# The causal mask of an attention stage: eight identity matmuls a head on TensorE, or adds by VectorE in PSUM

## The reference, cut to what matters

```python
q = rope(x @ w_q.T);  k = rope(x @ w_k.T);  v = x @ w_v.T
att = einsum('bqhd,bkhd->bhqk', q, k) / sqrt(64)
causal = tril(ones((S, S)))          # S = 1024
att = softmax(where(causal, att, -inf))
y = einsum('bhqk,bkhd->bqhd', att, v);  t = t + y @ w_o.T
```

## Time and profile before

| what | value |
|---|---|
| median of 3 runs | 4111.8 us (4111.73 to 4115.04) |
| the profiled execution | 4112.04 us, span 4110.2 us |
| TensorE busy | 3286.9 us (80%), 21207 matmuls |
| VectorE busy | 2073.0 us (50%) |
| ScalarE busy | 1432.6 us (35%) |
| GpSimd busy | 1538.1 us (37%) |
| attention stage, first to last mask matmul | 1105.3 to 3300.4 us |

### The profile page before, as it was taken

How to read it: one execution, slowest core, us unless ns; L and a number is a source line. 1 busy time by engine, 2 the same in 40 slices (tenths; PEclk the granted TensorE clock), 3 DMA queues, 4 the chain that set the end, 5 groups by cost and what they waited for, 6 DMA issues and landing times. The chain is left out here.

```text
span 4110.2 us, 65594 instructions
## 1 busy us (share of the span) xinstructions
PE 3286.9 (80%) x21207; PEld 2369.0 (58%) x21207; DVE 2073.0 (50%) x3068; ACT 1432.6 (35%) x2244; POOL 1538.1 (37%) x1314
## 2 busy tenths in 40 slices
PE   5333333333599999999999999999999939999998
PEld 1122222222366666666666666666666629898988
DVE  2344344344555555555555555555555555565656
ACT  0000000001144444444444444444444425454545
POOL 0577777777233333333333333333333320000000
PEclk8555555555699999999999999999999969999999
DMA  3533333333455555555545455555455533343333
GB/s 85 151 94 92 91 92 92 92 91 94 120 126 121 125 122 123 124 123 124 123 122 126 122 123 124 123 124 123 122 125 122 123 95 116 108 136 109 134 108 108
DMA packets 277334, 472.28 MB, mean 115 GB/s; under 512 B 91529, under 2 KB 103833, under 8 KB 277017
## 3 DMA queue, kind: packets, MB, share of 16 engines
q1 hardware_dynamic: 249624, 395.85, 37.2%
q0 software_dynamic: 27648, 75.53, 6.2%
HBM read 243.92 MB, written 22.29 MB: 65 GB/s over the span
## 5 line engine op out<-in xcount | busy, mean ns | idle before, releaser
L1034 ACT ACTIVATE attention_probs<-attention_pss 128x896 f32<-128x896 f32 (+4 forms) x768 | 621.3, 809 | 1003.7 <-PE attention_pss L901 994.2
L412 POOL DMA_INDIRECT deform_gat<-table,deform_idx x576 | 670.5, 1164 | 208.0 <-issue 164.2
L1083 DVE TENSOR_REDUCE attention_mx<-attention_pss 128x2 f32<-128x1024 f32 (+3 forms) x520 | 520.6, 1023 | 333.0 <-PE attention_pss L923 188.0
L967 PE MATMUL attention_psY<-attention_probs,attention_xt 128*64 128x64 f32 (+7 forms) x4386 | 645.7, 408 | 0.2 <-issue 0.2
L898 PE MATMUL attention_pss<-attention_QA,attention_KA 128*128 128x512 f32 (+4 forms) x1536 | 542.0, 407 | 15.9 <-ACT attention_probs L1034 12.0
L1121 POOL TENSOR_TENSOR attention_qk<-attention_tA,attention_tB 128x512 f32<-128x512 f32 x260 | 333.8, 1284 | 543.3 <-DVE attention_tB L1098 527.7
L1541 DVE SCALAR_TENSOR_TENSOR spectral_eo<-spectral_psE,spectral_sig,spectral_eo 64x512 fp32r<-64x512 f32 x512 | 383.9, 750 | 263.8 <-ACT spectral_eo L1520 259.2
L1444 PE MATMUL spectral_psE<-spectral_tz,spectral_up 128*128 128x256 f32 (+2 forms) x3072 | 507.5, 324 | 4.6 <-DVE spectral_eo L1541 4.6
L1444 PEld LDWEIGHTS spectral_psE<-spectral_tz,spectral_up 128*128 128x128 f32 x3072 | 470.6, 188 | 45.1 <-DVE spectral_eo L1541 6.3
L480 PE MATMUL deform_psT<-kept_ident,deform_smp 128*128 128x128 f32 (+1 forms) x320 | 85.0, 431 | 479.8 <-DVE deform_smp L439 479.8
L1097 DVE TENSOR_TENSOR attention_tA<-attention_pss,attention_cosT 128x512 f32<-128x512 f32 x260 | 179.2, 689 | 552.4 <-PE attention_pss L937 463.8
(11 more groups left out here) (164 smaller groups left out, 3747.4 us busy)
## 6 DMA issues: line engine op xcount, KB each, us to landing
attention_QA<-attention_nat_h SPq DMA_DIRECT2D x520, 128.0 KB, 2.3
spectral_tz<-phis SPq DMA_DIRECT2D x128, 320.5 KB, 4.6
spectral_tz<-phis SPq DMA_DIRECT2D x128, 320.0 KB, 4.2
attention_xb<-xn SPq DMA_DIRECT2D x67, 512.0 KB, 3.5
attention_wt<-wsplit SPq DMA_DIRECT2D x67, 512.0 KB, 4.2
attention_KA<-attention_nat_h SPq DMA_DIRECT2D x260, 128.0 KB, 2.3
attention_KB<-attention_nat_h SPq DMA_DIRECT2D x260, 128.0 KB, 2.3
attention_KA<-attention_nat_l SPq DMA_DIRECT2D x260, 128.0 KB, 2.3
```

The lines of the kernel that those rows point to most:

```text
L412: pool.indirect_dma_start(gat[:, r, k, :, :].rearrange("p q c -> p (q c)"), None, d.table.rearrange("r q c -> r (q c)"), bass.IndirectOffs ...
L967: ins = pe.matmul(psY[C * half:C * half + C, c0:c1], xt[:, kt_, :], probs[:, q + c0:q + c1], start=first, stop=(j == NS - 1), skip_group_c ...
L1034: act.activation(probs[:, pstep[j]:pstep[j] + width], pss[:, slot, lead:lead + width], ACT.Exp, scale=float(E) ** -0.5).then_inc(s_act, 1)
L1083: ins = dve.tensor_reduce(mx_far[:, :, i - 4] if k0 else mx[:, :, i], scores, AX.X, ALU.max)
```

## The change

VectorE adds the mask into the diagonal block of each tile, in PSUM, after the products of the unit are complete. A new semaphore `s_masked` counts the steps, and ScalarE's exponential waits for it in place of `s_full`. The mask matmuls on TensorE go away. The mask matmuls of the "max" units (L923) stay.

```diff
+        s_masked = sem("masked")
...
                                 for p0, p1 in by_bank(c0, c1):
-                                    pe.matmul(out[:, p0:p1], kt[:, h, P * kt_:P * kt_ + P],
+                                    ins = pe.matmul(out[:, p0:p1], kt[:, h, P * kt_:P * kt_ + P],
                                               qt[:, h, q0 + p0 - c0:q0 + p1 - c0], start=(a == 0), stop=(a == 1))
-                            d0 = c0 + P * kt_ - q0
-                            ins = pe.matmul(out[:, d0:d0 + P], identb[:, :], mask_b[:, 0, :], start=False, stop=True,
-                                            skip_group_check=True)
...
                         lead, _ = columns(j)
-                        act.wait_ge(s_full, n + 1)
+                        act.wait_ge(s_masked, BODY_HEADS * NS * it + NS * h + j + 1)
...
-                    if u[0] not in BY_ACT:
+                    if u[0] not in BY_ACT or u[0] == "S":
                         dve.wait_ge(s_full, n + 1)
+                    if u[0] == "S":
+                        for kt, q0, c0, _ in columns(u[1])[1]:
+                            d0 = c0 + P * kt - q0
+                            diagonal = pss[:, slot, d0:d0 + P]
+                            ins = dve.tensor_tensor(diagonal, diagonal, mask_b[:, 0, :], ALU.add)
+                        ins.then_inc(s_masked, 1)
```

## The result

The changed kernel takes 4042.86 us (median of 4 runs, 4042.79 to 4043.32) against 4111.76 for the kernel before in the same series. The ratio is 0.9831, 95% interval 0.9814 to 0.9848: 69 us faster, where 50 were forecast; the time lies in the stated range.

What follows compares the result with a forecast made beforehand. TensorE sets the pace. Masks save 1.52 us for two heads, less 0.35 (step 3 of the even head), 0.33 (pass start) and 0.07 (end of two heads): 0.77, 64 times 49.6, so 4112.0 becomes 4062; range 4030 to 4100.

Steps and rivals of the forecast that it cites:

- The masks' worth: TensorE without 1024 mask matmuls: 0.12 us saved before a same-shape matmul, 0.07 otherwise; 1.52 for two heads, 97 in all.
- The add: VectorE's 1024 adds of 128x128 in PSUM: 0.29 us each, bounds 0.21 and 0.42.
- The delay of the exponential: ScalarE's exponential starts 0.29 us later behind a one-tile step, at most 0.58 behind a two-tile step.
- step 3 of the even head: Score buffer refill there has slack 0.29 us: mask savings of 0.31 lost, plus 0.04, so 0.35 for two heads.
- the two places that I had seen at the edge: Steps 0 and 3 of the odd head: slack 0.44 and 0.55 us, 0.08 and 0.00 left, nothing lost.
- The start of a pass: Step 0 of a pass's first head: table load leaves no slack; 0.65 us lost for four heads, 0.33 for two.
- The end of two heads: Next scores wait up to 1.09 us for the maxima row's DMA; one mask's saving lost, 0.07 us for two heads.
- the second: Rival, 16%: VectorE's add takes its upper bound, 0.42 us; 25 us saved, 4087.
- the third: Rival, 7%: the exponential becomes the pace at score buffer reuse; kernel 35 us slower, 4147.
- the fourth: Rival, 5%: masks worth little, 0.04 us each, fitting into a stall that stays; 15 us left, or 4109.
- the fifth: Rival, 2%: TensorE's clock falls as it waits more often for buffers; some 220 us added, 4280.
- the first: Rival, 6%: the delay is hidden everywhere, so all 97 us are kept; 4015.

Runs made afterwards that it cites:

- e1: Kernel before, masks still on TensorE, with ScalarE's wait for s_pv put ahead of its wait for the scores: 4105.41 us against 4113.63.
- e6: Kernel before with the 1024 score masks left out, no adds, and ScalarE's s_pv wait ahead of the scores wait (timing only): 4008.51 us, ratio 0.9742.
- e4: Changed kernel with a second VectorE add of the same shape, into a spare SBUF tile, ahead of each add: 4072.66 us, ratio 0.9901.
- e5: Changed kernel with the mask of step 3 of the even heads (64 of 1024) back on TensorE: 4029.68 us, ratio 0.9794.
- e2: Changed kernel with the table load at the start of a pass put back behind the scores and add: 4069.42 us, ratio 0.9893.
- e7: Changed kernel with TensorE's waits at the head of a pass spread over the first three units: 4019.50 us, ratio 0.9769.
- e9: Kernel before, masks on TensorE, with ScalarE's s_pv wait first and TensorE's pass-head waits spread out: 4092.48 us, ratio 0.9951.
- e3: Kernel before with the 1024 score masks left out, no adds, waits unchanged (timing only): 4025.78 us, ratio 0.9785.

## Why the prediction was right, point by point

- **The masks' worth**: 0.12 us before a matmul of the same shape, 0.07 otherwise, 97 us in all. The total is confirmed by e1 against e6 (97 us), and the prices are borne out place by place: in the traces the stretch of the two-tile step 1 with its rope unit behind it is shorter by 0.25 in e6, that of a one-tile step ahead of a max unit by 0.06 to 0.08.
- **The add**: 0.29 forecast, 0.297 measured. Of the two figures of the Trainium skill, "VectorE: DVE Perf Modes", section on the TRN2 errata, the one for an fp32 add, 0.29 us, agrees; 120 + FD cycles, 0.26 us, does not.
- **The delay of the exponential**: mis-sized. I had set the earlier end of the scores equal to the hop to ScalarE. For step 0 of the odd head the exponential came 0.82 us after the first product of KB and QB before (2428.32 to 2429.14) and comes 1.00 after it now (2386.60 to 2387.60): 0.18 later, not 0.29. In the kernel before, 0.34 passed from the start of the mask to the exponential; now the add starts about 0.20 after the last score matmul has streamed, and the hand-over to ScalarE takes 0.03 to 0.04. The scores are ready for the reader earlier by more than the hundredths that I had taken. At step 3 of the even head it is 0.25 (2421.14 to 2421.89 before, 2379.43 to 2380.43 now): there the rope product is still in the way, by 0.07, where I had added 0.04. So the two places that I had seen at the edge kept 0.10 and 0.18 us between the end of the exponential and the refill (step 3 and step 0 of the odd head, 2395.59 to 2395.69 and 2388.62 to 2388.80); the longer delay of e4 used that up.

Those rows, of before and of after (timeline):

```profile
2421.14 0.57 PE L898 MATMUL attention_pss<-attention_QB,attention_KB 128*128 128x448 f32 x2
```

```profile
2386.60 0.63 PE L899 MATMUL attention_pss<-attention_QB,attention_KB 128*128 128x512 f32 x2
...
2387.60 1.02 ACT L1032 ACTIVATE attention_probs<-attention_pss 128x1024 f32<-128x1024 f32 x1 [1.50 <-DVE attention_pss L1081]
```

- **Step 3 of the even head**: 0.35 us for two heads lost. Right: the stretch takes 2.49 us, as before the change (2.48), e5 gets 0.23 of it back.
- **The start of a pass**: wrong, and this is the step that makes the most of the difference. "There is no slack: the whole 0.29 shows" took for granted that the table load stays behind the scores. A load that the compiler places went with the waits, and the change gave it another one. Forecast: 0.65 us a pass lost. Measured, by e2 against the changed kernel: 0.83 of such a loss avoided, 27 us, where 21 had been forecast; and the kernel before had lost 8 us at this place already (e1).
- **The end of two heads**: the wait named was wrong. Rows 8 gave 1.09 us to a DMA; the matmul row beside it, which I had not read, gives 0.42 to ScalarE's exponential:

```profile
2409.61 0.73 PE L898 MATMUL attention_pss<-attention_QA,attention_KA 128*128 128x512 f32 x2 [0.42 <-ACT attention_probs L1034]
```

  At the loop head line 1004 (L1002 in the changed kernel) waits for all of ScalarE's work. That happens once a pass, and there the delay of the last add shows in full; at the other pair nothing is lost, and the mask between is saved. Forecast 0.07 for two heads, 0.14 a pass; the pass end alone now holds 0.8 (e7: 23 us for 32 passes is 0.73), part of which stood there before (e9 against e1: 12 us, 0.37 a pass). So the change added some 0.36 a pass, 11 us, against 4.5 forecast.

The sum then closes: 97 for the masks, plus 8 for the table load (e1), minus 22 for step 3 (0.35 x 64), minus 11 for the pass end, is 72 us; 69 were measured. The losses can be checked at one stroke: e6 has neither masks nor adds, and its table load stands behind the wait for `s_pv` as in the changed kernel. Stretch by stretch (medians over the passes, from the first matmul of one kind to the first of the next) the two traces agree within 0.01 us but for two places. From the first score of step 3 of an even head to the matmuls of `pv` behind max-d TensorE takes 2.68 us in e6 and 3.04 in the changed kernel; from the last `pv` group of a pass to the next scores, 1.36 and 1.70. That is 2 x 0.36 + 0.34 = 1.06 a pass, 34 us, and 34 us lie between the medians (4008.51 and 4042.86).

The size was in part luck. 48 us of loss were forecast, 21 of them at a place where nothing was lost; instead 8 us were gained there, and the pass end lost 6 more than forecast. That the time lies in the range says little about the start of a pass: e2, where the load is on the path, lies in it as well (4069).

Of the rivals, the second (an add of 0.42), the third, the fourth and the fifth (clock 1.00 in every window read) did not come; the first, delay hidden everywhere, came half true: in all places but the two named above.

## What to carry to other kernels

When a wait moves, look at what the compiler has put between the waits of that instruction: a table load of 1.28 us sat behind the wrong one here and cost 8 to 27 us by its place alone (e1 8, e3 against e6 17, e2 27). A delay is priced place by place, slack against delay, and where one buffer has no slack the old way can stay for that one. At a loop head, ask whether the wait for "everything of the pass before" is what the first unit needs.

## What the runs showed of the hardware

- VectorE adds of 128x128 in a row start 0.20 us apart, although each is recorded with 0.29 (e4, 2399.49 to 2399.69 to 2399.89); the two adds of a two-tile step in the changed kernel take 0.50 together (2380.85). The second costs a third less than the first.
- From VectorE's end to ScalarE's start passed 0.03 to 0.04 us (2380.40 to 2380.43, 2370.14 to 2370.18). From the start of the matmul behind the last score matmul to the add it was 0.20 (2369.64 to 2369.84).
- A table load starts 0.01 to 0.02 us behind the exponential before it and the exponential behind it can start 0.02 after its end: 1.28 us in all (e7, 2354.72 to 2354.73 and 2356.01 to 2356.03).
- A wait named on the weight-load row can be a wait that costs nothing: e7 shows 0.60 us on it beside a matmul row without idle time.
